# Four fused graph layers on one core: one-hot matrices, early loads, the epsilon of the norms and the order around the second feed-forward product

## The reference

```python
# layer 0: attention over the adjacency, then a feed-forward part
q, k, v = x @ Wq + bq, x @ Wk + bk, x @ Wv + bv          # 8 heads of 64
attn = softmax(where(adj == 0, -1e9, q k^T / 8), over the heads)
h1 = layer_norm(x + (attn v) @ Wo + bo) * g1 + be1
h2 = layer_norm(h1 + relu(h1 @ W1 + b1) @ W2 + b2) * g2 + be2
x = norm(x + h2)
# layer 1: an edge network
h = mish(concat(x[src], x[dst], edge_attr) @ W1 + b1)     # 4096 x 1088 -> 512
messages = mish(h @ W2 + b2)
agg = segment_sum(messages, dst)
x = norm(x + layer_norm(x + mish(concat(x, agg) @ W3 + b3) @ W4 + b4))
# layers 2 and 3: two graph convolutions, then self and neighbour weights, norms after each
```

## Time and profile before

| | us |
|---|---|
| median of 3 runs | 247.41 |
| lowest and highest | 247.07 to 248.42 |
| profiled execution | 247.02 |
| its span | 245.2 |
| around the span | 1.8 |
| TensorE products busy | 230.8 (94% of the span) |
| VectorE busy | 153.8 (63%) |
| ScalarE busy | 123.5 (50%) |
| granted TensorE clock, mean over the span | 0.991 of full speed |

### The profile page before, as it was taken

One profiled execution on the slowest core, in us unless ns is written; L12 is line 12 of the kernel. 1 busy time (PEld: TensorE's weight loads), 2 busy tenths in 40 slices (PEclk: granted clock), 3 DMA queues, 4 the chain that ended last, 5 costly groups with the idle time before them and its releaser, 6 DMA issues.

```text
span 245.2 us, 3285 instructions
## 1 busy us (share of the span) xinstructions
PE 230.8 (94%) x1263; PEld 187.0 (76%) x1263; DVE 153.8 (63%) x268; ACT 123.5 (50%) x227; POOL 5.6 (2%) x17
## 2 busy tenths in 40 slices
PE   7998999988999999999999999999999999998980
PEld 4966879765676788888888888888888889996760
DVE  2979766337479656775855947758659454374625
ACT  0415289767929943755735546557355343244000
POOL 0000000000000000000000000000000000000001
PEclk9999999999999999999999999999999999999996
DMA  7999995500480000008022040040000000000001
GB/s 229 294 415 406 408 326 212 174 1 0 153 275 2 0 0 0 3 0 317 25 78 96 0 172 4 0 171 0 0 3 0 0 0 3 0 0 0 3 0 44
DMA packets 12991, 23.39 MB, mean 95 GB/s; under 512 B 920, under 2 KB 3888, under 8 KB 12848
## 3 DMA queue, kind: packets, MB, share of 16 engines
q1 hardware_dynamic: 12192, 22.68, 25.9%
q10 hardware_dynamic: 784, 0.50, 0.7%
HBM read 22.92 MB, written 0.26 MB: 95 GB/s over the span
## 4 chain that ended last, share of the span: by engine, by line
PE 84%; DVE 7%; ACT 4%; issue 2%; POOL 1%; POOLq 0%; DVEq 0%; ACTq 0%
PE bank L644 36%; PE bank L627 12%; PE bank L449 9%; PE bank L458 6%; PE bank L505 4%; PE bank L654 3%; PE bank L655 3%; ACT C L282 2%; DVE Sbf L854 2%; DVE Dbf L854 2%; PE bank L438 1%; PE bank L480 1%; PE bank L468 1%; PE bank L432 1%; ACT DT L296 1%
## 5 line engine op out<-in xcount | busy, mean ns | idle before, releaser
L644 PE MATMUL bank<-W2hi,Hhi 128*128 128x512 f32 x128 | 49.8, 389 | 0.0
L644 PE MATMUL bank<-W2hi,Clo 128*128 128x512 f32 x128 | 49.8, 389 | 0.0
L644 PE MATMUL bank<-W2lo,Hhi 128*128 128x512 f32 x128 | 49.8, 389 | 0.0
L366 ACT ACTIVATE Mhi<-M 128x512 fp32r<-128x512 f32 x32 | 20.2, 632 | 45.4 <-DVE M L961 45.4
L966 DVE TENSOR_TENSOR Mlo<-M,Mhi 128x512 fp32r<-128x512 f32 x32 | 22.1, 690 | 24.4 <-ACT M L367 24.4
L961 DVE TENSOR_TENSOR M<-bank,b2r 128x512 f32<-128x512 f32 x32 | 22.0, 687 | 12.6 <-PE bank L655 7.6
L644 PEld LDWEIGHTS bank<-W2hi,Hhi 128*128 128x128 f32 x128 | 24.0, 188 | 5.0
L644 PEld LDWEIGHTS bank<-W2hi,Clo 128*128 128x128 f32 x128 | 24.0, 188 | 5.0
L644 PEld LDWEIGHTS bank<-W2lo,Hhi 128*128 128x128 f32 x128 | 24.0, 188 | 5.0
L359 ACT ACTIVATE Hhi<-C 128x512 fp32r<-128x512 f32 x32 | 20.0, 624 | 12.4 <-DVE C L947 12.1
L947 DVE TENSOR_TENSOR C<-bank,C 128x512 f32<-128x512 f32 x32 | 21.4, 689 | 5.1 <-PE bank L627 4.1
(11 more groups left out here) (191 smaller groups left out, 316.6 us busy)
## 6 DMA issues: line engine op xcount, KB each, us to landing
F<-in_L_gnn_W SPq DMA_DIRECT2D x2, 2048.0 KB, 13.5
W1raw<-in_L_gnn_W SPq DMA_DIRECT2D x1, 2048.0 KB, 17.2
W<-in_L_gnn_W SPq DMA_DIRECT2D x1, 2048.0 KB, 9.0
Wq<-in_L_gnn_Wq SPq DMA_DIRECT2D x2, 512.0 KB, 4.4
Wk<-in_L_gnn_Wk SPq DMA_DIRECT2D x2, 512.0 KB, 7.8
Wv<-in_L_gnn_Wv SPq DMA_DIRECT2D x1, 1024.0 KB, 11.8
ea<-in_edge_attr SPq DMA_DIRECT2D x1, 1024.0 KB, 14.4
Wo<-in_L_gnn_Wo SPq DMA_DIRECT2D x1, 1024.0 KB, 16.1
```

The costliest lines, as they stand in the source:

```text
L366: act.activation(Mhi[:, t, :], M[:, t, :], ACT.Mish)
L644: done = mm(ST2[t][:, :], x[:, c, e], w[:, c, :], start=c == 0 and i == 0, stop=c == KC - 1 and i == 2)
```

## The change

Five edits:

1. **Loads.** `Wq` and `Wk` come in four row blocks each (128 x 512 floats, whole rows of 2 KB), and TensorE takes each block as it lands. The row `bo` goes behind `Wv` and `bv`. The rows `b2`, `g2` and `be2` go behind `F2`. The scores no longer stand behind eight edge counts; all 32 counts follow V.
2. **One-hots.** `Dbf` and `Sbf` are compared in bf16, from index tables held twice in a row (`dcol_twice`, `scol_twice`) and a bf16 copy of the number row (`numbers`), so that the innermost run of each operand is two elements.
3. **Source one-hots on VectorE.** `ST` is no longer turned on TensorE. The source indices are loaded to all partitions (`ids0`, `ids1`, 1 MB each, after `F2`), and eight `tensor_scalar` instructions compare them with the partition number. Each makes 512 columns; it reads every 32nd index. The eight groups of `turn_onehots` on `Sbf` and the eight ScalarE copies are gone, and edge steps 0 to 2 stand in their place.
4. **Smaller moves.** ScalarE copies the first score bank; GpSimd adds `xw`; features 0 and the first group of `DT` are turned ahead of the attention product; the first half of the product with `F2` is finished first, with one edge step after three parts and one after six in each half.
5. **Epsilon.** `stats` gets a third part, set once: all zero but for a spread of EPS * D. `bn_aggr` then reads three parts (two for one run of statistics), and `with_epsilon` is gone from all eight norms.

```diff
-        stats = sb("stats", [P, 2, 6])
+        stats = sb("stats", [P, 3, 6])
...
+                        ("ids0", 48, 4, I32), ("ids1", 87, 4, I32), ("Wclo", 77, 1, F32R), ("xhi", 78, 1, F32R), ("xlo", 79, 1, F32R))
...
+        ST_by_tile = ST.rearrange("p (q o i s e) -> p q s i o e", q=PAIRS, o=2, i=GT, s=2)
+        row_ids = [other[f"ids{h}"].rearrange("p (e q i o) -> p q i o e", q=PAIRS, o=2, i=GT) for h in range(2)]
...
-        DT_UNIT, ST_UNIT, C_UNIT = 0, G, 2 * G
+        DT_UNIT, C_UNIT = 0, G
...
# SyncE
-            for h in range(2):
-                sp.dma_start(Wq[:, :, D // 2 * h:D // 2 * (h + 1)], w_view(a["L0_gnn_Wq"])[:, :, D // 2 * h:D // 2 * (h + 1)]).then_inc(S[f"wq_in{h}"], 16)
...
+            for c in range(KC):
+                sp.dma_start(Wq[:, c, :], a["L0_gnn_Wq"][P * c:P * (c + 1), :]).then_inc(S[f"wq_in{c}"], 16)
+            for c in range(KC):
+                sp.dma_start(Wk[:, c, :], a["L0_gnn_Wk"][P * c:P * (c + 1), :]).then_inc(S[f"wk_in{c}"], 16)
...
+            sp.dma_start(W1raw, w_view(a["L1_gnn_W1"][0:2 * D, :])).then_inc(S["w1_in"], 16)
+            sp.wait_ge(S["pre_done"], C_UNIT)
+            sp.wait_ge(S["ct_done"], 1)
+            sp.dma_start(F2, w_view(a["L0_gnn_W2"])).then_inc(S["f2_in"], 16)
+            sp.wait_ge(S["wo_done"], 2)
+            for h in range(2):
+                sp.dma_start(other[f"ids{h}"], by_partition(a["src"][E // 2 * h:E // 2 * (h + 1)], E // 2)).then_inc(S[f"row_ids_in{h}"], 16)
             for name in EARLY_ROWS[4:]:
                 load_row(name)
...
# GpSimd
+            pool.wait_ge(S["x_in"], 16)
+            pool.wait_ge(row_in["L0_gnn_bo"], 16)
+            pool.tensor_tensor(xw[:, :], xs[:, :], row["L0_gnn_bo"], ALU.add).then_inc(S["xw_ready"], 1)
...
# ScalarE
+            act.wait_ge(S["scores_done"], 1)
+            act.activation(y[:, :], bank[1][:, :], ACT.Copy).then_inc(S["s_copied"], 1)
...
             for i in range(4):
                 w1_high(i)
                 relu_out(i)
-                onehot_out(ST, ST_UNIT, 2 * i)
-                onehot_out(ST, ST_UNIT, 2 * i + 1)
+                if i >= 1:
+                    edge_term_out(range(i - 1, i))
             features_high(3)
-            edge_term_out(range(RING_STEPS))
+            edge_term_out(range(3, RING_STEPS))
             act.wait_ge(S["w2_in"], 16)
+            act.wait_ge(S["st_ready"], 2 * PAIRS)
...
# TensorE
+            def features_as_loaded(banks, w, arrived, signal):
+                per = KC // len(banks)
+                for c in range(KC):
+                    pe.wait_ge(S[f"{arrived}{c}"], 16)
+                    for j in range(KC):
+                        done = mm(quarter(banks[j // per], j), w[:, c, P * j:P * (j + 1)], xT[:, c, :],
+                                  start=c == 0 and j % per == 0, stop=c == KC - 1 and j % per == per - 1)
+                        if c == KC - 1 and j % per == per - 1:
+                            done.then_inc(signal, 1)
...
-            count_edges(range(8))
-            pe.wait_ge(S["qk_ready"], 2 * KC)
...
+                    pe.wait_ge(S["qk_ready"], KC + j + 1)
...
+            count_edges(range(ET)).then_inc(S["ct_done"], 1)
...
                 features_by(F1_BANKS[i], 2 * i, (2 * i, 2 * i + 1), F1, xT, KC, S["f1_done"])
-                turn_onehots(Sbf, ST_UNIT, (2 * i, 2 * i + 1))
+                if i >= 1:
+                    edge_term(range(i - 1, i))
...
+            for h in range(2):
+                columns_by((bank[1], bank[2]), ffT, F2, h, range(0, 3), 0, FC - 1)
+                edge_term(range(2 * h + 3, 2 * h + 4))
+                columns_by((bank[1], bank[2]), ffT, F2, h, range(3, FC - 2), 0, FC - 1)
+                edge_term(range(2 * h + 4, 2 * h + 5))
...
                 columns_by((bank[1], bank[2]), ffT, F2, h, range(FC - 2, FC), 0, FC - 1).then_inc(S["f2_done"], 1)
...
+            edge_term(range(7, RING_STEPS - 1))
...
# VectorE
+            chain(v.memset(stats[:, 2, :], 0.0))
+            chain(v.memset(stats[:, 2, 2:3], EPS * D))
...
+            for ids, twice in ((dcol, dcol_twice), (scol, scol_twice)):
+                v.tensor_copy(twice[:, :, :], ids[:, :].unsqueeze(2).to_broadcast([P, ET, 2])).then_inc(S["ids_twice"], 1)
...
+            for twice, one in ((dcol_twice, Dbf), (scol_twice, Sbf)):
+                v.tensor_tensor(one.rearrange("p t (n k) -> p t n k", k=2), twice[:, :, :].unsqueeze(2).to_broadcast([P, ET, N // 2, 2]),
+                                numbers.rearrange("p (n k) -> p n k", k=2).unsqueeze(1).to_broadcast([P, ET, N // 2, 2]),
+                                ALU.is_equal).then_inc(S["onehot_bf"], 1)
...
+            def source_onehots(h):
+                dve.wait_ge(S[f"row_ids_in{h}"], 16)
+                for q in range(PAIRS):
+                    v.tensor_scalar(ST_by_tile[:, q, h], row_ids[h][:, q], iota_col[:, 0:1], None, ALU.is_equal).then_inc(S["st_ready"], 1)
+            source_onehots(0)
             dve.wait_ge(S["graphT_done"], 1)
...
+            source_onehots(1)
```

More of the change, by code:

```diff
@@ L514, in _ @@
             pe.wait_ge(S["xT_ready"], 1)
-            for h in range(2):
-                pe.wait_ge(S[f"wq_in{h}"], 16)
-                features_by(bank[2], 0, (2 * h, 2 * h + 1), Wq, xT, KC, S["q_done"] if h else None)
+            def features_as_loaded(banks, w, arrived, signal):
[7 more added lines that the diff above has]
+                            done.then_inc(signal, 1)
+            features_as_loaded((bank[2],), Wq, "wq_in", S["q_done"])
             pe.wait_ge(S["vecs_in"], 16 * len(COLS))
             nc.tensor.transpose(bank[7][:, 0:24], rowvecs[:, :], ident[0:24, 0:24]).then_inc(S["cols_done"], 1)
-            for h in range(2):
-                pe.wait_ge(S[f"wk_in{h}"], 16)
-                features_by(bank[3 + h], 0, (2 * h, 2 * h + 1), Wk, xT, KC, S["k_done"])
+            features_as_loaded((bank[3], bank[4]), Wk, "wk_in", S["k_done"])
             def count_edges(tiles):
@@ L527, in count_edges @@
                 return done
-            pe.wait_ge(S["onehot_bf"], 2)
-            count_edges(range(8))
-            pe.wait_ge(S["qk_ready"], 2 * KC)
-            for h in range(HEADS):
-                o, j = h % 2, h // 2
+            for o in range(2):
                 part = slice(HEAD * o, HEAD * (o + 1))
-                done = mm(quarter(bank[1 + o], j), kT[part, j, :], qT[part, j, :], start=True, stop=True)
-            done.then_inc(S["scores_done"], 1)
+                for j in range(KC):
+                    pe.wait_ge(S["qk_ready"], KC + j + 1)
+                    done = mm(quarter(bank[1 + o], j), kT[part, j, :], qT[part, j, :], start=True, stop=True)
+                done.then_inc(S["scores_done"], 1)
             pe.wait_ge(S["wv_in"], 16)
             nodes_by(bank[3], xT, Wv, S["v_done"])
-            count_edges(range(8, ET)).then_inc(S["ct_done"], 1)
+            pe.wait_ge(S["onehot_bf"], 2)
+            count_edges(range(ET)).then_inc(S["ct_done"], 1)
             pe.wait_ge(S["xw_ready"], 1)
@@ L549, in _ @@
                 mm(quarter(bank[3], j), v_sb[:, P * j:P * (j + 1)], uniform[:, :], start=j == 0, stop=False)
+            pe.wait_ge(S["ea_in"], 16)
+            turn_features(0)
+            pe.wait_ge(S["ident_bf_ready"], 1)
+            turn_onehots(Dbf, DT_UNIT, range(1))
             for o, j in ((o, j) for o in range(2) for j in range(KC)):
@@ L564, in _ @@
                         done.then_inc(S["wo_done"], 1)
-            pe.wait_ge(S["ident_bf_ready"], 1)
             pe.wait_ge(S["cols_ready"], 1)
             pe.wait_ge(S["ct_read"], 1)
-            turn_onehots(Dbf, DT_UNIT, range(G))
+            turn_onehots(Dbf, DT_UNIT, range(1, G))
             pe.wait_ge(S["ea_lo"], 1)
@@ L864, in features_low @@
                 v.tensor_tensor(EATlo[:, q, :], EA_BANKS[q][:, :], EAThi[:, q, :].bitcast(F32), ALU.subtract).then_inc(S["ea_lo"], 1)
[L866 to L868 removed]
+            dve.wait_ge(S["scores_done"], 2)
+            dve.wait_ge(S["s_copied"], 1)
             chain(v.tensor_tensor(y[:, :], bank[2][:, :], y[:, :], ALU.max))
```

58 lines of the change are left out of this document (19 added, 39 removed).

## The result

| | before | with the change |
|---|---|---|
| median, us | 247.48 (4 runs) | 245.41 (4 runs) |
| lowest and highest | 247.07 to 248.42 | 244.83 to 245.73 |
| profiled execution, its span | 247.02, 245.2 | 245.73, 243.8 |
| TensorE / VectorE / ScalarE busy | 230.8 / 153.8 / 123.5 | 230.8 / 153.4 / 120.6 |

The account below looks back on a forecast made before the run. TensorE bounds the main loop (busy 134.94 of 134.96 us), so gains lie ahead of it and in the tail: 2.05 + 0.45 - 0.1 = 2.4 us off 247.02 gives 244.6, plus 0.39 for a median of 245.0; range 243.4 to 247.6.

Parts of the forecast that it names:

- The place of the gain: Main loop untouched; all gain lies ahead of it and in the tail, with W1's product 2.05 us earlier, at 62.35.
- The scores at 14.9: Front: scores follow the K biases directly, with the counts behind V, and end at about 14.9, one microsecond earlier.
- V to the attention product: Front: 6.8 us of work, about 0.5 of counts and 0.7 of features and DT; attention product near 22.9 to 23.2.
- F1 at 32.8, a gain of 1.2 us: End of the front: the turn starts near 31.6 and the F1 product at 32.8 in place of 34.03.
- `xw` covered on GpSimd: Front: the sum on GpSimd, between 0.69 us and three times that, is covered, being first read near 20.6.
- F1 to F2's end: Stage ahead of the residual: 23.2 us by pieces against 23.27 before, a gain of about 0.1, ending at 56.05.
- the rival that they are cheap: F2's pieces run on without the 0.2 us per switch: stage 1.3 us better, total 243.8; chance 0.13.
- Residual and norm: Behind F2: from the residual's second half to the first half of xs, 4.75 us in place of 4.91.
- Source one-hots: Eight VectorE compares at 0.69 us each leave VectorE ready at 55.9, just in front of 56.05: cost zero.
- The rival of dear reads: Strided index reads at 1.38 us per compare make VectorE ready at 60.1, total 249.0; chance 0.10.
- V's weight late: Rival in the front: V's weight lands late, V starts 0.8 later, the front's 0.7 is gone: 245.7; chance 0.12.
- Epsilon 0.45: Tail: dropping the epsilon step, on the path in three of six norms, gains 0.45 us net of longer aggregates.

Follow-up runs that it names:

- the repeat: The changed kernel timed a second time with no edit: 245.37 us, ratio 0.9927 to the kernel before.
- e1: The kernel before with only the source one-hots on VectorE and the new order of F1 and F2: 246.12 us, ratio 0.9955.
- e7: The changed kernel with 12 of the 32 edge counts put back between K's product and the scores: 245.32 us, ratio 0.9927.
- e5: The changed kernel with the one-hot tables compared on 32-bit numbers as before: 245.23 us, ratio 0.9926.
- e8: The changed kernel with two warming products ahead of Q in place of four: 245.54 us, ratio 0.9928.
- e11: The changed kernel with the F2 product in its old order, two edge steps behind each half's first six parts: 244.69 us, ratio 0.9898.
- e2: The changed kernel with the old back (source one-hots on TensorE, old order around F2) and old epsilon, so only the new front: 247.19 us, ratio 1.0009.
- e6: The changed kernel with the source compares reading their 512 indices side by side, which changes the values: 244.8 us in one execution.
- e9: The changed kernel with each of the eight source one-hot compares made twice: 250.66 us, ratio 1.0135.
- e3: The kernel before with only the epsilon changed, by the third part of `stats`: 247.22 us, ratio 0.9998.

## Why the prediction was right, and where it was not

- **The place of the gain: right.** The main loop kept its pace; 1.2 of the 1.4 us in the span lie ahead of W1.
- **The scores at 14.9: wrong**, 16.12 in the first profile and 15.72 in the repeat. This is the term that was mis-sized, and the front hangs on it. "The scores follow the biases directly" had K's end at 13.67 and 0.56 us from the last bias to the end of the scores. In the first profile K ended 0.57 later, and V started 1.15 us behind the last bias. K's end: the late rise of the clock was not in the trace of before as a cost, since the wait for `Sbf` covered it (e1 shows it covered), and with a quick start the row blocks bind (the repeat). The 1.15: the new order of heads leaves all of the second half, eight products one at a time, behind the last bias; e7 shows them slow without any wait for a bias. No run has the changed kernel with the old order of heads, so the 0.55 us is read from rows of two kernels. The step that did not ask was edit 4: it takes a copy of 0.69 us off VectorE by an order that costs TensorE 0.55.
- **V to the attention product: right.** 8.0 us of work were counted (14.9 to 22.9); in e5, e8 and e11, where nothing is waited for, it is 7.91. Before it was 7.92 with 1.06 of waiting, so the old wait is filled and nothing is won in this piece.
- **From the attention product to F1: right**, 9.78 us against 10.27 before, 0.49 less.
- **F1 at 32.8, a gain of 1.2 us: wrong.** 34.12, and 33.26 to 34.05 in the other profiles with the new front, against 34.03 and 34.22 with the old one. By e2 the front alone can't be told from zero, by the repeat's profile it gives 0.37. What comes earlier comes to rest at the next wait: K's product for its row blocks, VectorE for V, TensorE for VectorE (e7).
- **`xw` covered on GpSimd: wrong in kind, small in size.** In most profiles it stretched one fold of VectorE's to 1.0 to 1.5 us, in e8 and e11 hardly, by the moment at which `bo` lands. The attention product waited for VectorE by 0.19 to 0.28 us in four profiles of this front and not at all in e5, e8 and e11, so it owes the sum at most that.
- **Compare speed without worth: right** (e5). **W1raw not binding: right.** It landed at 34.7, 22.5 us behind its issue and 0.9 earlier than before, and ScalarE's first high part followed at 34.9.
- **F1 to F2's end: the mechanism right, the size off by 0.6 us.** 22.58 measured for 23.2, with no ScalarE wait. The forecast has two accounts that do not meet: what goes out and comes in, taken from the 23.27 before (1.8 and 1.4 out, 0.9 and 1.3 in), gives 22.3, the pieces 23.1; it went by the pieces, and the measured stage lies between. The switches were priced at 0.2 us each, and e11 shows 0.21: the rival that they are cheap is out. What no step asked is whether they were needed; I took the split as given and never priced the old order with the new one-hots, which is 0.8 us shorter.
- **Residual and norm: 4.75 counted, 4.81 measured** from the residual's second half to the first half of xs. The second half started 0.11 us behind F2's end (0.05 counted), and the turn 0.14 behind the first half of xs, which had been counted at nothing; from the turn to W1 it was 1.49, as before.
- **Source one-hots: right.** 0.69 counted, 0.676 measured; VectorE ready at 56.24, 0.46 ahead of F2's end at 56.70. The rival of dear reads is out by e6: the step adds 0.195 us, not 0.7. The Trainium skill (Vector Engine (DVE) Microarchitecture Reference, § 5.1 and § 5.2) has both halves of this, two streams for one source in SBUF and a penalty for single elements; the trace agrees with the two together (0.676 us, half of the 1.4 that had been estimated for one stream). Doubling the price (e9) shows what such reads would have done to the total.
- **V's weight late: not what held V, but by luck.** It landed at 15.40 (14.4 to 15.4 in the profiles of this front), ahead of the scores' end. Had the scores ended at 14.9 as forecast, V would have stood there for 0.5 us: the forecast's own V at 14.9 was not to be had in this execution.
- **Epsilon 0.45: 0.25 measured** (e3), while the aggregate grows by 0.03 us on each norm, so part of the steps must have been covered; in the time it can't be told from nothing.

In sum, for the first pair of profiles: 1.2 us of front that did not come, 0.6 more from the stage, 0.2 less in the tail and 0.25 less between F2's end and W1 leave 1.4 of the 2.4 us. The medians stand 1.8 to 2.1 apart, since the executions with an earlier rise of the clock get about 0.4 us out of the front. So the total came near by luck: errors of opposite sign, of which none was foreseen.

## What to carry to other kernels

When loops are turned round to free another engine early, look at how the products then follow each other: here heads in alternate halves of the rows went two by two, heads of the same half one by one, and the scores grew by 0.55 us for a copy of 0.69 us taken off VectorE. When loads are cut into row blocks so that a product can start early, ask when the last block lands: K's product ended between 13.5 and 14.4 us in the profiles, with two column halves at 13.67. Before costing an earlier stage as a gain, follow it to the next meeting of engines; with two paths of nearly one length a microsecond taken off one only becomes a wait. And when an order mixes two kinds of product to give a third engine an early start, price the switches, and look whether that engine is free to take the early half when it comes.

## What the runs showed of the hardware

- Four warming products of 512 columns at the start took 1.34, 1.91, 1.03, 1.85 and 1.66 us in executions of nearly the same program. In the chain of waits they fill 1.71 us in the first profile and 0.86 in the repeat, which is four times 512 columns at the lower level of the clock (1.2 GHz) and at the higher (2.4 GHz). So the moment of the rise moves by about a microsecond or more from one execution to the next, while the profile's granted clock reads 1.00 there; only the durations tell.
- Products that use 64 rows started two by two when they took the two halves of the rows in turn (16 in 1.16 us), and one by one when eight of one half followed each other (16 in 1.71 us with no operand to wait for, e7).
- GpSimd adding 128x512 numbers (1.26 to 1.37 us) stretched VectorE's fold of 256 columns from 0.42 to 1.44 us, and in the repeat the one of 128 columns from 0.29 to 1.24: VectorE stood for nearly the whole time.
- A single-source compare of 512 columns took 0.481 us read side by side and 0.676 with a step of 32 numbers.
- A change between the products of 512 columns from 64 rows and those of 256 columns from 128 rows costs TensorE 0.21 us with nothing to wait for (e11 against the changed kernel, a mean over four changes).
